# Ranking and degree columns by accumulating instructions, and 56 of 196 payload columns scattered a stage earlier

## What is computed

```python
# first layer (SAGE), x: (50000, 128)
neigh_sum = segment_sum(x[src], dst, num_segments=N)
deg = segment_sum(ones, dst, num_segments=N)
h = concatenate([x, neigh_sum / maximum(deg, 1.0)[:, None]], axis=1) @ W_neigh + b_neigh
x = _layernorm(x + h)
# second layer (two GCN steps): the degree counts a self loop too
dis = rsqrt(deg + 1)
h = segment_sum((dis[row] * dis[col])[:, None] * x[col], row, num_segments=N)   # row = src, col = dst
```

## Time and profile before

| | us |
|---|---|
| runs | 5191.07, 5186.94, 5193.55 |
| median | 5191.07 |
| profiled execution | 5192.05 |
| its span in the profile | 5190.1 |

### The profile page before, as it was taken

One profiled execution on the slowest core, in us unless ns is written; L12 is line 12 of the kernel. 1 busy time (PEld: TensorE's weight loads), 2 busy tenths in 40 slices (PEclk: granted clock), 3 DMA queues, 4 the chain that ended last, 5 costly groups with the idle time before them and its releaser, 6 DMA issues. The chain is left out here.

```text
span 5190.1 us, 95540 instructions
## 1 busy us (share of the span) xinstructions
PE 3396.3 (65%) x21145; PEld 2503.1 (48%) x21146; DVE 3401.2 (66%) x12799; ACT 2337.2 (45%) x6751; POOL 3490.4 (67%) x4335
## 2 busy tenths in 40 slices
PE   0566776777778699969949999941001999431566
PEld 0465665676756344422236667631000777321566
DVE  6996666544468577668848888851441888642776
ACT  0343665676757444423338888820000444100466
POOL 3760886777735577726758888867575555673999
PEclk9988999999989899979979999965555999755788
DMA  2332665888899742101124444443112999352576
GB/s 76 103 119 97 203 206 170 247 258 243 262 238 282 246 138 53 53 20 35 38 73 142 144 140 139 145 125 96 33 41 88 295 293 292 119 148 55 168 225 198
DMA packets 593106, 784.81 MB, mean 151 GB/s; under 512 B 138946, under 2 KB 362870, under 8 KB 592330
## 3 DMA queue, kind: packets, MB, share of 16 engines
q1 hardware_dynamic: 431734, 533.20, 33.2%
q0 software_dynamic: 62848, 112.43, 8.9%
q10 hardware_dynamic: 98328, 137.22, 7.2%
HBM read 470.23 MB, written 317.95 MB: 152 GB/s over the span
## 5 line engine op out<-in xcount | busy, mean ns | idle before, releaser
L2902 POOL TENSOR_SCALAR n_hot<-node_of,d_krel 128x256 f32<-128x256 f32 x396 | 381.1, 976 | 65.2 <-ACTq L2958 65.2
L1350 ACT ACTIVATE n_r<-n_r,n_shift,n_rstd 128x128 f32<-128x128 f32 x784 | 321.6, 480 | 79.4 <-POOL n_shift L1341 73.4
L2930 PE MATMUL n_bank<-h_rows,n_hot 128*128 x1584 | 239.2, 319 | 145.4 <-POOL n_hot L2902 144.4
L998 POOL DMA_INDIRECT x_rows<-x,d_other_i x196 | 237.1, 1210 | 118.8 <-POOLq L102 59.4
L684 POOL DMA_INDIRECT agg<-e_msg,e_put_i x196 | 194.8, 994 | 165.4 <-DVEq L713 114.1
L2930 PEld LDWEIGHTS n_bank<-h_rows,n_hot 128*128 128x128 f32 x1584 | 226.8, 230 | 158.5 <-issue 158.5
L1350 ACT ACTIVATE n_o<-n_y_ps,n_shift,n_rstd 128x128 f32<-128x128 f32 x784 | 292.6, 453 | 16.9 <-POOL n_shift L1637 16.8
L1057 PE MATMUL e_bank<-x_rows,e_hot 128*128 x1584 | 225.3, 310 | 91.6 <-DVE e_hot L1013 77.1
L1057 PEld LDWEIGHTS e_bank<-x_rows,e_hot 128*128 128x128 f32 x1584 | 216.8, 221 | 100.4 <-issue 100.4
L615 POOL DMA_INDIRECT agg_dst<-e_rows,e_put_i x196 | 195.2, 996 | 102.0 <-issue 59.4
L2523 POOL TENSOR_TENSOR n_u<-n_u 128x512 f32<-128x512 f32 x98 | 124.5, 1271 | 206.0 <-DVE n_u L2470 206.0
(11 more groups left out here) (522 smaller groups left out, 11625.1 us busy)
## 6 DMA issues: line engine op xcount, KB each, us to landing
n_ag<-agg_dst SPq DMA_DIRECT2D x196, 264.0 KB, 2.9
n_hs<-h SPq DMA_DIRECT2D x196, 264.0 KB
n_xs<-x SPq DMA_DIRECT2D x196, 256.0 KB, 4.2
agg_dst<-e_ev SPq DMA_DIRECT2D x196, 132.0 KB
y<-n_o ACTq DMA_DIRECT2D x98, 264.0 KB, 2.8
e1a_fed<-y SPq DMA_DIRECT2D x196, 132.0 KB
m<-e1a_ev SPq DMA_DIRECT2D x196, 132.0 KB
e1b_fed<-m SPq DMA_DIRECT2D x196, 132.0 KB
```

The source lines that it names most:

```text
L998: pool.indirect_dma_start(out=rows[:, c, 0:fetched], out_offset=None, in_=table, in_offset=bass.IndirectOffsetOnAxis(ap=e.other_i[:, c:c + ...
L1350: ins = act.activation(out[:, g, 0:D], r[:, g, :], ACT.Identity, bias=shift[:, g:g + 1], scale=rstd[:, g:g + 1])
L2902: ins = pool.tensor_scalar(hot[:, i // STEPB % HOTS, i % STEPB, :], keep.node_of[:, :], e.krel[:, i:i + 1], None, ALU.is_equal)
L2930: ins = pe.matmul(bank[:, bass.ds(to + h * 256, SUMMED)], hot[:, s, k, h * P:(h + 1) * P], flat_rows[:, bass.ds(row, SUMMED)], start=False ...
```

## The change

Counting and ranking no longer run in rounds of seven columns. `count_digits` is 196 `tensor_scalar` compares of 196 bf16 elements, each with its sum written to one column of the histogram (`accum_out`). `find_places` is one `scalar_tensor_tensor` per edge column: digit equal, times a row `adds` that holds the bases and then ones, with the sum written to the place. A batch now ranks four columns, from batch 2 to batch 50. After the first 56 columns the places are converted, and GpSimd, when it has issued all gathers of the first walk, scatters these 56 columns (`scatter_early`). In the node pass three columns are scattered for every two blocks.

The degree columns start at 1, 11/9, 0 and 0 and grow by 1, 2/9, 1 and 0 with every edge, so a tile's columns hold deg + 1, 1 + (deg + 1) x 2/9 and deg. In the node pass `degree` is gone; `factor` is one product, two steps after the load instead of four; VectorE takes the maximum with 1 of two columns at once. SP's load of a block now also waits for `added`, the factor of the block six before.

```diff
-FEW = 7
+FEW, FOUND = 4, 4
+EARLY = 56
 PLACES_FROM = 2
 ...
-        self.link(dve.tensor_copy(self.dig, self.key_i[:, :]))
+        dve.tensor_copy(self.dig[:, :], self.key_i[:, :])
+        self.link(dve.tensor_copy(self.beside[:, digits:digits + J], self.key_i[:, :]))
+    def count_digits(self, dve):
+        for d in range(HIGH):
+            if d >= FOUND:
+                dve.wait_ge(self.counted, d - FOUND + 1)
+            dve.tensor_scalar(self.found[:, d % FOUND, 0:J], self.beside[:, HIGH:HIGH + J], float(d), None, ALU.is_equal, ALU.add,
+                              accum_out=self.hist[:, d:d + 1]).then_inc(self.counted, 1)
 ...
     def find_places(self, dve, c):
+        for k in range(c, c + FEW):
+            if k >= FOUND:
+                dve.wait_ge(self.summed, k - FOUND + 1)
+            dve.scalar_tensor_tensor(self.found[:, k % FOUND, 0:HIGH + k], self.beside[:, 0:HIGH + k], self.dig[:, k:k + 1],
+                                     self.adds[:, 0:HIGH + k], ALU.is_equal, ALU.mult, accum_out=self.place[:, k:k + 1])                .then_inc(self.summed, 1)
+        if c + FEW in (EARLY, J):
+            first = 0 if c + FEW == EARLY else EARLY
+            dve.wait_ge(self.summed, c + FEW)
+            dve.tensor_copy(self.place_i[:, first:c + FEW], self.place[:, first:c + FEW]).then_inc(self.placed, 1)
+    def scatter_early(self, pool):
+        pool.wait_ge(self.placed, 1)
+        for c in range(EARLY):
+            if c >= 8:
+                pool.wait_ge(self.put[c % 8], 16 * (c // 8))
+            self.scatter(pool, c, self.put[c % 8])
+        for n in range(8):
+            pool.wait_ge(self.put[n], 16 * EARLY // 8)
 ...
 # walk: GpSimd, after the last gather
                 landed(J // 4 - 1)
+                if by_source is not None:
+                    by_source.scatter_early(pool)
 # walk: VectorE
-                    if b >= PLACES_FROM and (b - PLACES_FROM) % 2 == 0 and (b - PLACES_FROM) // 2 < J // FEW:
-                        by_source.find_places(dve, (b - PLACES_FROM) // 2 * FEW)
-                by_source.keep_places(dve)
+                    if 0 <= b - PLACES_FROM < J // FEW:
+                        by_source.find_places(dve, (b - PLACES_FROM) * FEW)
 # FromZero
+    DEGREES = (1.0, 1.0), (11.0 / 9.0, 2.0 / 9.0), (0.0, 1.0), (0.0, 0.0)
+        for i, (first, each) in enumerate(self.DEGREES):
+            dve.memset(self.zeros[:, :, D + i:D + i + 1], first).then_inc(self.zeroed, 1)
+            dve.memset(rows[:, :, D + i:D + i + 1], each)
 # node_sage: SP, GpSimd, VectorE
                     sp.wait_ge(turned[s], used)
+                    sp.wait_ge(added[s], used)
                     sp.dma_start(ag[:, s], block_rows(agg, turn, s)).then_inc(ag_in[s], 16)
-                    pool.tensor_tensor(q[:, s, 0, :], ag[:, s, :, D], keep.ones[:, 0:GB], ALU.add).then_inc(counted[s], 1)
 ...
+                    done(pool, ag_in, turn, s, 16)
                     free(pool, stored, turn, s, 16)
-                    pool.tensor_tensor(o[:, s, :, D + 1], part[:, s, :], q[:, s, 0, :], ALU.mult).then_inc(added[s], 1)
+                    pool.tensor_tensor(o[:, s, :, D + 1], ag[:, s, :, D + 1], ag[:, s, :, D], ALU.mult).then_inc(added[s], 1)
 ...
-                    for i in range(2):
-                        k = (turn * SLOT + s) * 2 + i
+                    for k in range(3 * n // 2, 3 * (n + 1) // 2):
 ...
+                            by_source.scatter(pool, EARLY + k, sorted_in[k % 8])
-                pipeline(pool, (0, degree), (4, factor), (0, sort), written_out=True)
+                pipeline(pool, (2, factor), (0, sort), written_out=True)
 ...
-                    st(dve.tensor_scalar(q[:, s, 1, :], ag[:, s, :, D], 1.0, None, ALU.max))
-                    done(dve, counted, turn, s)
+                    free(dve, sums_ready, turn, s)
+                    st(dve.tensor_scalar(q[:, s], ag[:, s, :, D:ROW:2].rearrange("p g i -> p i g"), 1.0, None, ALU.max))
```

More of the change, by code:

```diff
@@ L895, in memory @@
         self.keep, self.total_ps, self.before_ps = keep, total_ps, before_ps
[L896 to L900, removed]
+        self.edges_in, self.key_i = ph.sb("ends", [P, WS, J], I32), ph.sb("key_i", [P, J], I32)
+        self.beside, self.dig = ph.sb("beside", [P, digits + J], BF16), ph.sb("dig", [P, J])
+        self.adds, self.found = ph.sb("adds", [P, digits + J]), ph.sb("found", [P, FOUND, digits + J], BF16)
+        self.hist, self.hist_h = ph.sb("hist", [P, digits]), ph.sb("hist_h", [P, digits], F16)
         self.one_row, self.total, self.place = ph.sb("one_row", [P, digits]), ph.sb("total", [P, digits]), ph.sb("place", [P, J])
+        self.base = self.adds[:, 0:digits]
         self.ends_in, self.loaded, self.chain = (ph.sem(n) for n in ("ends_in", "loaded", "chain"))
@@ L904, in memory @@
             ph.sem(n) for n in ("hist_ready", "sums_done", "sums_read", "placed"))
-        self.dig = self.beside[:, digits:digits + J]
+        self.counted, self.summed = ph.sem("counted"), ph.sem("summed")
+        self.put = [ph.sem(f"put{n}") for n in range(8)]
     def load(self, sp):
@@ L920, in find_digits @@
         dve.memset(self.one_row[:, :], 1.0)
-        dve.tensor_tensor(self.earlier[:, :, :], keep.iota_h[:, 0:FEW].unsqueeze(1).broadcast_to([P, FEW, FEW]),
-                          keep.iota_h[:, 0:FEW].unsqueeze(2).broadcast_to([P, FEW, FEW]), ALU.is_lt)
+        dve.memset(self.adds[:, digits:digits + J], 1.0)
         dve.tensor_copy(self.beside[:, 0:digits], keep.iota_h[:, 0:digits])
@@ L925, in find_digits @@
         self.link(dve.tensor_scalar(self.key_i[:, :], self.edges_in[:, 0, :], LOW.bit_length() - 1, None, ALU.logical_shift_right))
-        self.link(dve.tensor_copy(self.dig, self.key_i[:, :]))
[L928 to L935, removed]
+        dve.tensor_copy(self.dig[:, :], self.key_i[:, :])
[6 more added lines that the diff above has]
+                              accum_out=self.hist[:, d:d + 1]).then_inc(self.counted, 1)
+        dve.wait_ge(self.counted, HIGH)
+        dve.tensor_copy(self.hist_h[:, :], self.hist[:, :]).then_inc(self.hist_ready, 1)
     def sum_counts(self, pe):
@@ L1022, in _ @@
                 by_source.find_digits(dve)
-                for d in range(0, HIGH, FEW):
-                    by_source.count_digits(dve, d)
+                by_source.count_digits(dve)
                 by_source.find_base(dve)
@@ L1397, in node_sage @@
 def node_sage(nc, keep, x_turned, agg, w, bias, y1, by_source):
-    with Phase(nc, "n0", freed="turned added stored y_ready x1_ready sums_ready meaned inverted") as ph:
+    with Phase(nc, "n0", freed="turned added stored y_ready x1_ready inverted sums_ready") as ph:
         wa, wb, b, b_rest = ph.sb("wa", [P, D]), ph.sb("wb", [P, D]), ph.sb("b", [1, D]), ph.sb("b_rest", [1, D])
@@ L1448, in _, with factor @@
             def _(pool):
[L1449 to L1453 removed]
+                pool.wait_ge(cleared, 1)
+                def factor(turn, s):
                     done(pool, ag_in, turn, s, 16)
[L1455 to L1466 removed]
                     free(pool, stored, turn, s, 16)
[L1468 removed]
+                    pool.tensor_tensor(o[:, s, :, D + 1], ag[:, s, :, D + 1], ag[:, s, :, D], ALU.mult).then_inc(added[s], 1)
                 def sort(turn, s):
[L1472 to L1475 removed]
+                    n = turn * SLOT + s
+                    for k in range(3 * n // 2, 3 * (n + 1) // 2):
+                        if 8 <= k < J - EARLY + 8:
                             pool.wait_ge(sorted_in[k % 8], 16 * (k // 8))
[L1477 to L1481 removed]
+                        if k < J - EARLY:
+                            by_source.scatter(pool, EARLY + k, sorted_in[k % 8])
+                pipeline(pool, (2, factor), (0, sort), written_out=True)
+                for k in range(3 * NB // 2, J - EARLY + 8):
                     pool.wait_ge(sorted_in[k % 8], 16 * (k // 8))
@@ L1542, in _ @@
             def _(dve):
-                dve.memset(ninths[:, :], 2.0 / 9.0).then_inc(cleared, 1)
                 dve.memset(o[:, :, :, :], 0.0).then_inc(cleared, 1)
-                dve.wait_ge(cleared, 2)
+                dve.wait_ge(cleared, 1)
                 link = linked(dve, chain)
```

48 lines of the change are left out of this document (9 added, 39 removed).

## The result

The changed kernel takes 5033.25 us (median), beside 5189.0 us for the kernel before on the same chip; the ratio is 0.9701, 95% interval 0.9682 to 0.972. Its profiled execution took 5033.11 us, with a span of 5031.4 us. So it is 3% faster, and 5038 us was forecast. One of the changed kernel's four runs took 5789.74 us at a granted clock of 0.628, where the others have 0.865 to 0.867, and is left out of the ratio.

The account below looks back on a forecast made before the run. VectorE was taken to bound the walk and GpSimd to lead in the node pass. 5192.05 - 86 (walk) - 67 (node pass) = 5039, with the median 1.0 us under: 5038 us, range 5018 to 5060 (chance 0.62).

Parts of the forecast that it names:

- Counting: VectorE before the walk: 196 summing compares at 0.31 us, 60.8 us instead of 88.7; first one-hot at about 143 us.
- Ranking: VectorE in the walk: 196 instructions at 0.48 us, 94 us instead of 178.6; VectorE and TensorE through at 387 us.
- "Half rate": Rival, chance 0.09: ranking's summing three-operand form takes two steps per element, 0.79 us per column; 5087 us.
- "slower": Rival, chance 0.04: both summing forms run at several steps per element; at three times 1.045 ns, 5228 us.
- Gathers: GpSimd in the walk: 1.24 us each during counting, 1.31 beside ranking, instead of 1.51; they end at 326 us.
- "port": Rival, chance 0.12: ranking instructions hold GpSimd's gathers up as the old compares do; node pass starts at 446, 5083 us.
- The reading that the forecast leaned on: Scatters beside three-operand instructions have median and minimum 982 ns, so gathers seem to slip between short ranking instructions; 0.07 us added.
- Early scatters and the start: GpSimd after the gathers: 56 scatters at 1.28 us, 72 us, to 398; node pass starts at 403, 86 us gained.
- 5 us for the last landing and the change of phase: Between the early scatters' end at 398 us and the node pass's start at 403: 5 us added.
- Node pass: Node-pass blocks go from 3.845 to 3.15 us over 97 blocks, 67 us gained; the new SP wait costs nothing.
- the ring: Node pass, three output banks: two blocks pass per round from product to next product; 3.08 us a block, 3.15 taken.
- "Node pass": Rival, chance 0.12: scatters were not the last bound, or SP's new wait bites; blocks settle at 3.5 us, 5073 us.

Follow-up runs that it names:

- e4_six_banks: The changed kernel with six output banks of TensorE in the node pass instead of three; 5013.4 us.
- e8_marks: The changed kernel with two one-column GpSimd memsets as marks, behind the last early scatter and behind the waits for the last landings; 5027.65 us in one run.
- e2_degrees: The kernel before with the degree columns alone: old counting and ranking, two scatters a block, none early; 5114.98 us (ratio 0.9861).
- e3_ranking: The kernel before with the accumulating counting and ranking alone: old degree operations, two scatters a block, none early; 5090.98 us (ratio 0.9818).
- e1_no_early: The changed kernel without early scatters, all 196 columns at two to a block of the node pass; 5004.87 us.
- e7_seven: e1_no_early with seven ranked columns behind each batch of six one-hots instead of four; 5040.85 us.

## Why the prediction was right, step by step

- **Counting.** 0.31 us each was forecast. The timeline gives one every 0.28 us, just under the lower bound of 0.285:
```profile
75.70 0.08 DVE L935 DVE_READ_ACCUMULATOR e_found<-e_beside 128x1 f32 x1
75.70 0.35 DVE L935 TENSOR_SCALAR_CACHE_REDUCE e_found<-e_beside 128x196 bf16<-128x196 bf16 x1
75.98 0.08 DVE L935 DVE_READ_ACCUMULATOR e_found<-e_beside 128x1 f32 x1
75.98 0.35 DVE L935 TENSOR_SCALAR_CACHE_REDUCE e_found<-e_beside 128x196 bf16<-128x196 bf16 x1
```
  The 0.025 us set aside for the semaphore wait doesn't show; that the four buffers in turn hide it is argued and was not tried with fewer. Hence 54.4 us instead of 60.8. The first one-hot came 9 us before the forecast mark, 6 of them from here.
- **Ranking.** 0.48 us was forecast on average. At 196 elements one starts every 0.345 us, at 297 every 0.45:
```profile
139.98 0.41 DVE L961 SCALAR_TENSOR_TENSOR e_found<-e_beside,e_dig,e_adds 128x196 bf16<-128x196 bf16 x1
...
140.32 0.42 DVE L961 SCALAR_TENSOR_TENSOR e_found<-e_beside,e_dig,e_adds 128x197 bf16<-128x197 bf16 x1
...
233.31 0.52 DVE L961 SCALAR_TENSOR_TENSOR e_found<-e_beside,e_dig,e_adds 128x297 bf16<-128x297 bf16 x1
...
233.76 0.52 DVE L961 SCALAR_TENSOR_TENSOR e_found<-e_beside,e_dig,e_adds 128x298 bf16<-128x298 bf16 x1
```
  (0.45 - 0.345) / 101 is 1.04 ns per element, the slope that the earlier trace rows gave, and 0.14 us are fixed. At the mean width that is 0.447 us, 88 us in all against 94. (The prediction writes that the old compares began at 7 x 196 elements; the mean of 2082 that it reckons with is right, and belongs to 7 x 203 up to 7 x 392.) TensorE began its last product of the walk at 382.7 us; the end was forecast at 387.
- **"Half rate" and "slower"** fall by that slope. The Trainium skill, page "Vector Engine (DVE) Microarchitecture Reference", section "Points that are easy to get wrong", states half throughput for this kind of instruction with two SBUF sources that are not bf16. Here one source is bf16, and the measured full rate doesn't contradict it.
- **Gathers, and "port".** 1.24 us while counting and 1.31 beside ranking were forecast; the timeline has 1.25 and a mean of (321.6 - 134) / 147 = 1.28. The last gather starts at 321.6, so it ends 3 us ahead of the forecast 326. Beside the short ranking instructions most gathers take the 0.94 us of one that nothing delays, but not all. First the gathers by source (ns minimum/median/maximum, first and last start), then the longest in the timeline:
```profile
L1009 POOL DMA_INDIRECT x_rows<-x,d_other_i x196: 940/944/1251, 72.4 to 321.6; - x196
```
```profile
320.08 1.25 POOL L1009 DMA_INDIRECT x_rows<-x,d_other_i  x1 [0.30 <-issue]
```
  The delay has not gone, it has become short: 0.31 us at most, where the earlier trace rows show 0.74 and the longest gather before took 2.58 us. The rule in the Trainium skill's page "SBUF — State Buffer", section "Who interferes with whom", is that the loser waits until the other instruction has finished. These rows agree with it: the ranking instructions that run at 320 us are listed with 0.61 us, longer than any delay. The reading that the forecast leaned on was weak. The three-operand instructions of the stage with the scatters of the earlier trace rows are these, in the same form:
```profile
L639 DVE SCALAR_TENSOR_TENSOR e_rows<-e_rows,e_cont x195: 350/352/353, 3718.0 to 3826.6; 128x128 f32<-128x128 f32 x195
```
  The scatters start between 3721.2 and 3974.8, 116 of the 196 after the last of them, so the median of all says little; of the 80 begun before, 51 take 0.98 us, which agrees with the forecast's reading.
- **Early scatters and the start.** 1.28 us each, as forecast. The first began at 326.0, also as forecast, but by luck: the gathers were 3 us early, and 3.4 us of waiting, for which the forecast has no term, stand between the last gather and it. The trace puts that wait down to the second copy of places at 325.2, though the code asks there only for the first (made at 189.4). In e4_six_banks, which has the same walk, that copy came at 324.7 and the trace names the landing of the gathers:
```profile
326.39 1.01 POOL L979 DMA_INDIRECT by_src<-by_src_pay,by_src_place_i  x1 [3.06 <-DMA x_rows<-x,d_other_i]
```
  In the five kernels with early scatters the gap is 3.1 to 3.4 us wherever the copy falls, so it is the landing. The last scatter ended at 397.15 (398 forecast). The term that was mis-sized is "5 us for the last landing and the change of phase", for which the forecast names no row: it is 8.9, of which the landing is 1.2 (e8_marks). So the start is 406, not 403, a gain of 82.6 against 86. As GpSimd ended the walk, the 9 us by which counting and the 4 us by which TensorE came early gained nothing.
- **Node pass.** 3.15 us a block was forecast and 3.13 measured, and the ring that was named as next is what binds (e4_six_banks). Beyond the prediction the pass fills sooner: from its first transfer to its first store 30.6 us instead of 35.9. In e2_degrees it is 30.4 and in e3_ranking 36.0, so the degree operations on GpSimd had stood in the first block's chain. Together 74.7 against 67. "Node pass" falls.
- **The sum** came within 5 us because the two errors, 3 us short in the walk and 8 us over in the node pass, have opposite signs; that part of it is luck.

What the prediction had in hand and did not conclude: by its own terms GpSimd, with two scatters a block instead of one and a half, would have come to 2.3 + 0.64 = 2.94 us, under the 3.15 of the ring, while the 56 early scatters put the walk's end from 387 to 398. They could only cost. e1_no_early shows it: 22.6 us.

## What to carry to other kernels

Read each part of a change in its own stage, and ask of a part that moves work whether the place it leaves was still full after the other parts: here the degree columns had already emptied GpSimd in the node pass, so the scatters moved out of it only lengthened the walk. Where an engine with slack in one stage would be the last to finish another, leave the work where the slack is. Bound an unseen instruction form by slope and fixed part from rows of its relatives: here the ranking came out inside its bounds, and the counting 0.007 us under its lower one.

## What the runs showed of the hardware

- An instruction that sums into a column can be charged with less than its listed length when others of its kind surround it: 196 elements are listed with 0.35 us, but the next starts 0.28 us after it, with the 0.08 us reading of the sum beneath the next one's time.
- A gather that GpSimd issues in 0.94 us took up to 2.58 us beside the ranking of seven columns at a time and at most 1.25 us beside that of single columns (before and changed kernel).
- Ending a phase took about 7.5 us when GpSimd, with indirect transfers just landed, came to it last (398.14 to 405.6 in e8_marks). Where GpSimd had finished long before, the next stage's first transfer came 1.4 us after TensorE's last product (e1_no_early).
- TensorE's granted clock was 1.00 over the ranking stretch in the changed kernel, that is the upper of its levels, 2.4 GHz, throughout. It was 0.88 on average in the walk before and 0.90 in e7_seven's ranking stretch, where VectorE was busy without a break and TensorE 101 of 139 us; means between its two levels, so for part of the time it stood at the lower one, 1.2 GHz.
